# Norms split between VectorE and ScalarE, the last token tile transposed behind the first products, and the scan's head by halves, in a two-layer MLA, scan and MoE tower

## The reference

```python
h = tok(x, ...)                                   # (16, 37, 256): patches @ W + b, class token, positions
h = h + mla_attention(_layernorm(h), ...)         # l = 0: kv rank 64, q rank 128, 16 heads, rope 32, causal
h = h + moe_8_experts_top2(_layernorm(h), ...)    # l = 1: F = 1024, one shared expert
h = h + selective_scan(_layernorm(h), ...)        # l = 2
h = h + moe_64_experts_top8(_layernorm(h), ...)   # l = 3: F = 128, a shared expert of 256

def _layernorm(x, eps=1e-05):
    m = jnp.mean(x, axis=-1, keepdims=True)
    v = jnp.var(x, axis=-1, keepdims=True)
    return (x - m) / jnp.sqrt(v + eps)

# the scan; d = 256 channels, n = 16 states, u = x @ w_in
dt = softplus(x @ w_in @ w_x[:, :64] @ w_dt + b_dt) * (DT_MAX - DT_MIN) + DT_MIN
dA = dt[:, :, None] * A
h = exp(dA) * h + einsum('bdn,bn,bd->bn', dA, B_t, u_t)[:, None, :]
y = einsum('bdn,bn->bd', h, C_t) + Dp * u_t
```

## Time and profile before

| | us |
|---|---|
| runs | 449.02, 450.86, 452.77 |
| median | 450.86 |
| the profiled execution | 450.0 |
| its span on the core | 446.9 |
| TensorE busy | 413.4 (92%) |
| VectorE busy | 257.8 (58%) |
| GpSimd busy | 157.0 (35%) |
| ScalarE busy | 135.9 (30%) |
| mean DMA rate | 142 GB/s |

### The profile page before, as it was taken

The page is one execution under the profiler, slowest core; times in us unless marked ns, Lnnn a source line. Parts: engine busy times, 40 slices in busy tenths (PEclk is TensorE's granted clock), DMA queues, the critical chain, the costliest instruction groups (busy, mean ns, idle before and its releaser), DMA issues. The chain is left out here.

```text
span 446.9 us, 8837 instructions
## 1 busy us (share of the span) xinstructions
PE 413.4 (92%) x2990; PEld 330.8 (74%) x2990; DVE 257.8 (58%) x649; ACT 135.9 (30%) x343; POOL 157.0 (35%) x129
## 2 busy tenths in 40 slices
PE   8999999889981999999999899998998999999993
PEld 5665567766761999999986489886676788888872
DVE  0548878766930012211165789997776556656545
ACT  1030068783310111121202765552401132323210
POOL 2007835540075000100362068781001156554560
PEclk9999999999995899999999999999999999999997
DMA  8763086001085367786234033430124577777462
GB/s 269 223 182 104 2 291 229 3 1 56 1 304 219 111 224 233 276 286 227 59 99 146 24 143 104 109 83 2 54 55 141 163 174 202 179 186 186 109 128 100
DMA packets 32076, 63.55 MB, mean 142 GB/s; under 512 B 6062, under 2 KB 19677, under 8 KB 29741
## 3 DMA queue, kind: packets, MB, share of 16 engines
q1 hardware_dynamic: 26381, 50.90, 36.3%
q0 software_dynamic: 5664, 12.25, 10.7%
HBM read 50.51 MB, written 12.63 MB: 141 GB/s over the span
## 5 line engine op out<-in xcount | busy, mean ns | idle before, releaser
L1850 PE MATMUL PS<-xT,w1s 128*128 128x296 f32 x224 | 60.7, 415 | 0.0
L1850 PEld LDWEIGHTS PS<-xT,w1s 128*128 128x128 f32 x224 | 41.4, 190 | 11.1 <-issue 0.2
L1723 PE MATMUL PS<-scratch,w0up 128*128 128x144 f32 (+1 forms) x256 | 38.1, 310 | 12.0 <-DVE scratch L1153 11.6
L1723 PEld LDWEIGHTS PS<-scratch,w0up 128*128 128x128 f32 x256 | 36.4, 198 | 13.9 <-DVE scratch L1153 12.5
L1799 PE MATMUL PS<-ident,scratch 128*128 128x128 f32 (+1 forms) x340 | 43.9, 281 | 1.2 <-DVE scratch L1249 1.1
L617 POOL DMA_INDIRECT scratch<-xg,idx_nxt x18 | 17.9, 996 | 72.7 <-DVE idx_nxt L1382 38.7
L1799 PEld LDWEIGHTS PS<-ident,scratch 128*128 128x128 f32 (+1 forms) x340 | 38.8, 183 | 5.6 <-DVE scratch L1249 2.4
L1243 DVE TENSOR_TENSOR_SCAN scratch<-scratch,PS 128x592 f32<-128x592 f32 x32 | 41.9, 1362 | 1.4 <-PE PS L1806 1.4
L1170 DVE COPY scratch<-PS 128x144 f32<-128x144 f32 (+1 forms) x16 | 5.1, 321 | 64.7 <-PE PS L1732 64.7
L769 ACT ACTIVATE scratch<-PS 128x288 f32<-128x288 f32 (+1 forms) x32 | 13.8, 431 | 76.5 <-PE PS L1723 76.5
L1865 PE MATMUL PS<-w1s,scratch 128*128 128x256 f32 (+1 forms) x140 | 34.8, 382 | 2.0 <-DVE h L1286 1.1
(11 more groups left out here) (326 smaller groups left out, 752.2 us busy)
## 6 DMA issues: line engine op xcount, KB each, us to landing
w0dn<-in_w0dn SPq DMA_DIRECT2D x9, 1024.0 KB, 5.8
w0up<-in_w0up SPq DMA_DIRECT2D x9, 1024.0 KB, 6.1
w0dn<-in_w SPq DMA_DIRECT2D x16, 384.0 KB, 3.6
scratch<-rows_c SPq DMA_DIRECT2D x14, 296.0 KB, 3.3
by_expert<-zeros SPq DMA_DIRECT2D x2, 1920.0 KB, 13.3
w1s<-in_w SPq DMA_DIRECT2D x14, 256.0 KB
w1s<-in_w SPq DMA_DIRECT2D x14, 128.0 KB, 3.2
w0up<-in_patchesT SPq DMA_DIRECT2D x6, 296.0 KB, 4.3
```

The source lines that it names most:

```text
L1723: last = mm(PS[:, z, (f % 2) * width:(f % 2 + 1) * width], w0up[:, s, c, f * P:(f + 1) * P], xeT[:, s, c, 0:width], start=c == 0, stop=c == 1)
L1850: last = mm(PS[:, 2 * n + j, 0:HALF], w1s[:, s, w:w + F1], xT[:, c, half(n)], start=c == 0, stop=c == 1)
```

## The change

- **The norm on two engines.** VectorE normalises tiles 0, 1 and 4, ScalarE tiles 2 and 3 (Identity, scale `rstd`, bias `xshift` = -mean x rstd, which VectorE makes in a new instruction). Tile 4's statistics come after tiles 0 and 1. `xn_ready` counts three tiles a layer, and a new `xn_act` the two of ScalarE. At l = 3 both engines read PSUM; the copies into `h` come behind the norm, and the table with the square root is loaded after the scan by a square root with no use.
- **Tile 4 apart.** TensorE transposes tiles 0 to 3, starts on the sublayer's products, and transposes tile 4 in front of the first that need it. At l = 1 the transposes go to banks 2 and 3.
- **The scan's head.** dt's products of token half 0 for both channel halves, u's first product, tile 4's transposes, dt's of half 1, the rest of u. ScalarE does Abs, Exp, Abs, Exp. The two copies of u go, and VectorE reads u in PSUM.
- **A wait on GpSimd.** Its scatters of tiles 2 to 4 wait for `xeT_ready` 1, the copy of item 0's transposed rows (L1153 before).

The diff, without the declarations, joint 0's TensorE code (cut as joint 1's) and `stats_of`, a name for the statistics of one tile:

```diff
@@ -369,7 +370,16 @@
         LN_PARTS = ((0, 4), (4, NTILE))
-        XT_BANK = (0, 0, 0, 3)
+
+        def xn_landed(eng, l, t):
+            if t in (2, 3):
+                eng.wait_ge(xn_act, 2 * l + t - 1)
+            else:
+                eng.wait_ge(xn_ready, 3 * l + (3 if t == NTILE - 1 else t + 1))
+
+        def normed_from(l, t):
+            return h[:, t, :] if l < 3 else PS[:, t // 2, (t % 2) * D:(t % 2 + 1) * D]
+        XT_BANK = (0, 2, 0, 3)
@@ -547,6 +557,8 @@
             for t in range(NTILE):
+                if t == 2:
+                    pool.wait_ge(xeT_ready, 1)
@@ -654,15 +666,19 @@
 
-            def layernorm(l, keep_rows=None):
-                for p, (a, b) in enumerate(LN_PARTS):
-                    if keep_rows:
-                        keep_rows(p)
-                    act.wait_ge(var_ready, 2 * l + p + 1)
-                    nc.scalar.activation(std[:, a:b], mv[:, a:b, 1], ACT.Sqrt, bias=LN_EPS).then_inc(std_ready, 1)
+            def layernorm(l):
                 a, b = LN_PARTS[0]
+                act.wait_ge(var_ready, 2 * l + 1)
+                nc.scalar.activation(std[:, a:b], mv[:, a:b, 1], ACT.Sqrt, bias=LN_EPS).then_inc(std_ready, 1)
+                act.wait_ge(shift_ready, l + 1)
+                for t in (2, 3):
+                    nc.scalar.activation(xn[:, t, :], normed_from(l, t), ACT.Identity, bias=xshift[:, t:t + 1],
+                                         scale=rstd[:, t:t + 1]).then_inc(xn_act, 1)
...
                 nc.scalar.copy(xT[:, 1, a * P:b * P], PS[:, XT_BANK[l] + 1, 0:(b - a) * P]).then_inc(xT_hi, 1)
+                a, b = LN_PARTS[1]
+                act.wait_ge(var_ready, 2 * l + 2)
+                nc.scalar.activation(std[:, a:b], mv[:, a:b, 1], ACT.Sqrt, bias=LN_EPS).then_inc(std_ready, 1)
@@ -782,7 +798,6 @@
                                      bias=b_dt[:, c:c + 1]).then_inc(sp_abs, 1)
-            for c in range(2):
@@ -812,13 +827,13 @@
 
-            def keep_scanned(p):
-                for b in ((0, 1), (2,))[p]:
-                    n, rows = (2, P) if b < 2 else (1, ROWS[4])
-                    act.wait_ge(h_stats, b + 1)
-                    nc.scalar.copy(h[0:rows, 2 * b:2 * b + n, :].rearrange("p t d -> p (t d)"), PS[0:rows, b, 0:n * D]).then_inc(h_kept, 1)
-
-            layernorm(3, keep_scanned)
+            nc.scalar.activation(rms[:, :], ssq[:, :], ACT.Sqrt, bias=RMS_EPS, scale=1.0 / R_KV)
+            layernorm(3)
+            for b in range(3):
+                n, rows = (2, P) if b < 2 else (1, ROWS[4])
+                act.wait_ge(xn_ready, 3 * 3 + (2, 2, 3)[b])
+                nc.scalar.copy(h[0:rows, 2 * b:2 * b + n, :].rearrange("p t d -> p (t d)"), PS[0:rows, b, 0:n * D]).then_inc(h_kept, 1)
+
@@ -873,26 +888,33 @@
 
-            def layernorm(l, last_tile, kept=None):
+            def layernorm(l, last_tile, first_of_last=None):
                 settle()
-                for t in range(*LN_PARTS[0]):
+                a, b = LN_PARTS[0]
+                for t in range(a, b):
...
                 last.then_inc(var_ready, 1)
+                if first_of_last:
+                    first_of_last()
+                dve.wait_ge(std_ready, 2 * l + 1)
+                link(nc.vector.reciprocal(rstd[:, a:b], std[:, a:b]))
+                nc.vector.scalar_tensor_tensor(xshift[:, a:b], mv[:, a:b, 0], -1.0, rstd[:, a:b], ALU.mult,
+                                               ALU.mult).then_inc(shift_ready, 1)
+                def normalize(t):
+                    nc.vector.tensor_scalar(xn[:, t, :], normed_from(l, t), mv[:, t, 0:1], rstd[:, t:t + 1],
+                                            ALU.subtract, ALU.mult).then_inc(xn_ready, 1)
+
+                for t in (0, 1):
+                    normalize(t)
...
                 nc.vector.bn_aggr(mv[:, NTILE - 1, :], stats[:, NTILE - 1, :]).then_inc(var_ready, 1)
-                for p, (a, b) in enumerate(LN_PARTS):
-                    dve.wait_ge(std_ready, 2 * l + p + 1)
-                    link(nc.vector.reciprocal(rstd[:, a:b], std[:, a:b]))
-                    if kept:
-                        dve.wait_ge(h_kept, kept[p])
-                    for t in range(a, b):
-                        nc.vector.tensor_scalar(xn[:, t, :], h[:, t, :], mv[:, t, 0:1], rstd[:, t:t + 1],
-                                                ALU.subtract, ALU.mult).then_inc(xn_ready, 1)
-                a, b = LN_PARTS[0]
...
                 nc.vector.tensor_copy(xT[:, 0, a * P:b * P], PS[:, XT_BANK[l], 0:(b - a) * P]).then_inc(xT_lo, 1)
+                dve.wait_ge(std_ready, 2 * l + 2)
+                link(nc.vector.reciprocal(rstd[:, b:NTILE], std[:, b:NTILE]))
+                normalize(NTILE - 1)
@@ -1193,16 +1218,16 @@
             def close_tile(t):
-                if t in LATE:
-                    add_late(t)
                 add_routed(0, t)
-                step(nc.vector.bn_stats(stats[:, t, :], h[:, t, :]))
+                stats_of(t)
...
             for t in range(NTILE - 1):
+                if t in LATE:
+                    add_late(t)
                 close_tile(t)
-            layernorm(2, lambda: close_tile(NTILE - 1))
+            layernorm(2, lambda: close_tile(NTILE - 1), lambda: add_late(NTILE - 1))
@@ -1212,20 +1237,24 @@
             nc.vector.tensor_scalar(spb, spb, DT_MAX - DT_MIN, DT_MIN, ALU.mult, ALU.add).then_inc(sp_taken_max, 1)
-            for c in range(2):
+            def u_of(c):
                 dve.wait_ge(u_mm, c + 1)
-                nc.vector.tensor_copy(u[:, c, :].rearrange("p (b n) -> p b n", b=2), PS[:, 2 * c:2 * c + 2, 0:HALF]).then_inc(u_ready, 1)
+                return PS[:, 2 * c:2 * c + 2, 0:HALF]
+
+            def skip_term(c):
+                nc.vector.tensor_scalar(du[:, c, :].rearrange("p (b n) -> p b n", b=2), u_of(c), d_p[:, c:c + 1], None,
+                                        ALU.mult).then_inc(du_ready, 1)
+
+            skip_term(0)
...
                 dve.wait_ge(dt_ready, c + 1)
-                dve.wait_ge(u_ready, c + 1)
-                nc.vector.tensor_tensor(dtu[:, c, :], dt[:, c, :], u[:, c, :], ALU.mult).then_inc(dtu_ready, 1)
-            for c in range(2):
-                last = nc.vector.tensor_scalar(du[:, c, :], u[:, c, :], d_p[:, c:c + 1], None, ALU.mult)
-            last.then_inc(du_ready, 1)
+                nc.vector.tensor_tensor(dtu[:, c, :].rearrange("p (b n) -> p b n", b=2),
+                                        dt[:, c, :].rearrange("p (b n) -> p b n", b=2), u_of(c), ALU.mult).then_inc(dtu_ready, 1)
+            skip_term(1)
@@ -1287,6 +1316,7 @@
 
+            dve.wait_ge(h_kept, 3)
@@ -1442,15 +1472,14 @@
 
-            def transpose_xn(l, fill=0):
-                for t in range(NTILE):
-                    pe.wait_ge(xn_ready, NTILE * l + t + 1)
+            def transpose_xn(l, tiles, fill=0):
+                for t in tiles:
+                    xn_landed(pe, l, t)
...
                                                    xn[:, t, c * P:(c + 1) * P], ident[:, :])
-                    if t in (NTILE - 2, NTILE - 1):
-                        last.then_inc(xT_mm, 1)
+                last.then_inc(xT_mm, 1)
@@ -1651,9 +1682,11 @@
             keep_busy(7, 10)
-            transpose_xn(1, 5)
+            transpose_xn(1, range(NTILE - 1), 3)
...
             for t in range(NTILE):
+                if t == NTILE - 1:
+                    transpose_xn(1, (t,))
@@ -1759,19 +1792,26 @@
             pe.wait_ge(dtw_ready, 3)
-            transpose_xn(2, 4)
-            for c in range(2):
-                for n in range(2):
-                    if c == 0:
-                        need_xT(2, n)
+            transpose_xn(2, range(NTILE - 1), 3)
+            def make_u(c, n):
+                for k in range(2):
+                    last = mm(PS[:, 2 * c + n, 0:HALF], w_in[:, k, c * P:(c + 1) * P], xT[:, k, half(n)], start=k == 0, stop=k == 1)
+                return last
+
+            for n in range(2):
+                if n:
+                    make_u(0, 0)
+                    transpose_xn(2, (NTILE - 1,))
+                need_xT(2, n)
+                for c in range(2):
...
                                   start=k == 0, stop=k == 1)
-                last.then_inc(dt_mm, 1)
+                    if n:
+                        last.then_inc(dt_mm, 1)
             for c in range(2):
-                for n in range(2):
-                    for k in range(2):
-                        last = mm(PS[:, 2 * c + n, 0:HALF], w_in[:, k, c * P:(c + 1) * P], xT[:, k, half(n)], start=k == 0, stop=k == 1)
+                for n in range(c == 0, 2):
+                    last = make_u(c, n)
@@ -1787,7 +1827,7 @@
             def start_y():
-                pe.wait_ge(u_ready, 2)
+                pe.wait_ge(du_ready, 2)
@@ -1817,7 +1857,6 @@
             start_y()
-            pe.wait_ge(du_ready, 1)
@@ -1834,9 +1873,11 @@
             keep_busy(7, 13)
-            transpose_xn(3, 4)
```

(23 more changed lines are left out.)

## The result

| | before | changed |
|---|---|---|
| median | 451.40 | 442.78 |
| runs | 449.02 to 452.77 (4) | 442.35 to 444.28 (4) |
| profiled execution | 450.0 | 443.19 |
| its span | 446.9 | 441.5 |
| TensorE busy | 413.4 (92%) | 415.7 (94%) |

The median before is that of four runs here; 450.86, from which I forecast, was that of the first three. The ratio of the runs is 0.9857, with an interval of 0.9816 to 0.9898: faster by 1.4%. The forecast was 449.3 in a range of 441 to 453.5; the measured time lies in the range, but at rival B (443.5), not at the forecast.

The account below looks back on a forecast made before the run. It saw a chain of waits spread over many lines, with one large 10.5 us hold before item 0's copy. Joints +1.1 and hold -2.7 took profiled 450.0 to 448.4; with 0.9 for the median, 449.3, range 441 to 453.5.

Parts of the forecast that it names:

- rival B: At item 0's copy: the hold goes with the scatters' issuing; 8.5 us taken as gain, 443.5 in all; chance 0.25.
- The hold: 10.5 us between item 0's transposes' modelled end and VectorE's copy of their result, with the four compute engines doing nothing.
- if the release follows the landing of what was issued: At item 0's copy: six scatters fewer in flight ahead, so the copy comes 2.6 us earlier; 2.7 taken.
- A: The forecast itself: item 0's copy 2.7 us earlier, joints 1.1 us slower, 449.3 in all; chance 0.42.
- Case C: At item 0's copy: the hold stands unchanged and only the joints' cost remains, 452.0; chance 0.22.
- Case D: The hold stays for the weights and a second stop comes with the postponed scatters beside item 0's products, 454.7; chance 0.08.
- The joints: Four places where norm and transposes lead to the next products; the new order there costs +1.1 us together.
- joint 0: Transposes ahead of the kv products: earlier start and tile 4's later transposes cancel, change 0.
- Joint 1: Transposes ahead of the router's products, which lead to the gathers: the router ends 0.4 us later.
- Joint 2: Scan's head: the first Ln comes 1.9 us later, part given back by reading u in PSUM; sum +1.2 us.
- Joint 3: After the scan, up to the sigmoid: earlier table load and later copies of h let it start 0.5 us sooner.
- joint 1's detour: Tile 4's transposes and their copy between the router's early and last products, priced at 1.0 us.

## Why the prediction was right or wrong

**The hold: the right place, the wrong release.** The measured time, 442.78, lies 6.5 us under the forecast. It is in the range because I had drawn that wide enough for rival B, and not by my mechanism. The step that failed is "if the release follows the landing of what was issued", 2.6 us, which I took over rival B's 8.5. The trace of the change has the release under full DMA traffic (1.01, 35 packets of q0 among it), 1.7 behind the end of the last scatter's issue (1.7 in each of the three traces on chip 15), and 2.4, 2.6 and 2.7 with ten scatters. B's own sum, 7.6 earlier, came out as 7.2 in the case's traces and 8.3 on chip 15; counted from the transposes' end the hold is 8.3 and 8.4 shorter. B's further gain, 0.9 for the low clock behind the hold, was 0.5: item 0's up products take 7.15 after and 7.67 before, since the clock falls behind the short hold as well. I had both numbers, 140.84 and 143.2, in front of me in the earlier trace rows, and chose by the last packets of the earlier trace rows, which fell together with them. One trace could not tell the two apart, so B should have had no less than A; B had 0.25 and A 0.42. No row could have told me that the gain would be there on some chips only.

**The rule against it.** By "SBUF — State Buffer", section "Who interferes with whom", of the Trainium skill, transfers don't hold a compute engine. The runs agree in part: DMA at 1.01 did not keep the copy from starting, and on chips 5 and 0 nothing did. But in the case and on chips 15 and 8 the results of item 0's transposes reached VectorE 2.2 to 10.6 us behind their modelled end, while scatters were being issued and up to 2.7 behind them. No run shows whether what came late here was an access to SBUF at all. Case C, the hold that stands, fell.

**Case D** was right in one thing and wrong in the rest. The second stop exists, 0.9 us in one trace and 1.6 in three, and it is almost hidden: on chip 15 TensorE stood still for 0.2 to 0.3 behind it, where I had 2.7, since it had the down products of the earlier Gelus to do. But the first hold did not stay.

**The joints: +1.1 forecast, +2.1 and +2.6 measured** (the change without the wait on chips 5 and 8, by the ratios; the medians differ by 1.9 and 1.6). By terms, from the traces of before and after: joint 0, from the first aggregate of joint 0 to that of joint 1, 81.87 and 81.85, as forecast (0). Joint 1, to the router's result, 7.76 and 8.10: +0.34 for +0.4. Joint 2, to the first scan step, 22.19 and 23.49: +1.3 for +1.2. Joint 3, to the sigmoid, 6.83 and 6.12: -0.7 for -0.5. So every priced term held: +0.9 together.

Two things that I had at nothing are in the traces, both of them clock. Behind joint 1 it cost 1.3 in the traces of the case and of chip 5, and nothing on chips 15 and 8: from that aggregate to the first scatter it is 25.58 in the kernel before, 27.24 and 27.26 in the changed code with the lower clock, and 25.94, 25.94 and 25.93 without. At the start of the scan the granted clock fell as well, in the trace of the change:

```profile
252.00:255.00 3.00, 2.84 (x11) 1.91 (x11) 2.95 (x3) 2.16 (x4) 2.13 (x3) 0.79 0.28 84
255.00:258.00 3.00, 3.00 (x13) 2.38 (x12) 3.00 (x4) 2.76 (x4) 1.78 (x1) 0.64 0.66 194
```

The scan, from its first to its last step, took 48.84 instead of 47.53. All five traces of the changed code with joint 1's detour have 48.8 or more (50.47 once). But the kernel before with the wait at tile 0 or at tile 4 had 48.84 too, the one with the wait at tile 2 had 47.53 twice, and the changed kernel without the detours 47.27. So this can't be put down to the change, and how much of the cost on chip 8 it makes, where joint 1 lost no clock, stays open.

Two other points. I said that the fills hide the norm at joint 1, with ten of them in front; the transposes began 2.87 behind the aggregate, as before, so the claim held. The wait itself is free, as forecast, with the scatters of tiles 2 to 4 behind it, and stops being so with all ten.

**The ledger** of the two case profiles, in us: start to joint 0 -0.7, joint 0 0, joint 1 to the first scatter +1.7, from there to the copy -8.2, to joint 2 -0.6, joint 2 +1.3, the scan +1.2, joint 3 to the end -0.1: -5.4, the difference of the spans. The first entry is no gain: joint 0's aggregate starts at 21.04 and 20.30 in two traces of the kernel before, and at 20.36 in that of the change.

## What to carry to other kernels

A long wait for a result that by the trace had long been done was worth more here than all four joints; look for one in the groups by line, as a long idle time with its releaser ended well before. When a gap has two candidate causes that end within 2 us of each other, work out what the edit makes of each, and don't favour one for which the trace has nothing more to say. And measure a baseline on more than one chip before a gain is put down to code: here 2% of it exists on some chips only.

## What the runs showed of the hardware

- The same program took 436.7 to 438.4 us on three chips and 448.8 to 449.3 on two. The traces have one gap that goes with it: VectorE's copy of finished transposes started 10.5 us behind their modelled end, while GpSimd issued ten indirect scatters, and 2.2 us behind it with four. Why some chips do it is open, and so is what in the chip is late, the matmuls' true end or their signal. That it goes by GpSimd's issuing is argued from seven traces: the copy starts 2.4 to 2.7 us behind the last of ten and 1.7 behind the last of four, in the latter case with the scatters' own packets still moving on q0. Why the one is 1 us longer is open too.
- Scatters in issue beside running products did not hold back every result: in the four traces of the change with its wait that have the hold, one of four Gelus was late, by 0.9 us once and 1.6 three times.
- The same detour at joint 1, with a break of 0.52 us in TensorE's work, was followed by a granted clock of 0.50 in two of five traces and by the full clock in the other three.
- A product with one operand in PSUM (128x592) took 0.77, as from SBUF (0.78). ScalarE's normalising of two tiles took 1.09, the second beginning some 0.5 behind the first. VectorE's normalising of four tiles took 1.38 from SBUF and 1.90 from PSUM.
